# Product 2 of batch 0 moved in front of the rows of batch 2, in the hand-written order of an attention and expert kernel

## The chip, the cores and the metric

The kernel runs on one core of a Trainium2 chip. A core has five engines that run side by side, each through a queue of its own and in order: TensorE (PE, matrix products and transposes), VectorE (DVE), ScalarE (ACT), GpSimd (POOL) and SyncE (SP, which only issues transfers here). They meet through semaphores. The metric is the device time of one execution in microseconds; lower is better.

## The reference, cut to what matters

Four batches of 512 tokens with 512 features go through a normalisation, an int8-quantised two-layer block with weights of the batch's own, a residual, a second normalisation, and a mixture of 8 experts of which each token uses 2, with another residual.

```python
def _smooth_quant_linear(x, w):
    s = sqrt(max(amax_x, EPS) / max(amax_w, EPS))          # per column, over the rows
    xs, ws = x / s, w * s
    x_scale = max(max(abs(xs), axis=-1), EPS) / 127.0      # per row
    w_scale = max(max(abs(ws), axis=-1), EPS) / 127.0
    return round(xs / x_scale) @ round(ws / w_scale).T * x_scale * w_scale.T

def _expert_forward(xe, guw, dw):                          # batch b: guw 512x512, dw 512x256
    gate, up = split(_smooth_quant_linear(xe, guw), 2)     # product 1
    return _smooth_quant_linear(silu(gate) * up, dw)       # product 2

x = x + vmap(_expert_forward)(layernorm(x), w1, w2)
# then x + FFN(layernorm(x)): top 2 of 8 experts by router scores, f32, 512 -> 256 -> 512
```

## The kernel before

**Two parts on one time axis.** The first part quantises and multiplies each of the four batches. The second sorts the tokens by expert into 39 tiles of 128 rows, gathers each tile's rows, multiplies them by its expert's weights and adds the result to the output by an indirect transfer. The expert weights (8 experts, 3 matrices each, so 24 pieces numbered 0 to 23) come in while the first part runs. Each is loaded into one of three staging buffers ("load expert k" on SyncE), its high half is written as f16 by ScalarE ("high k", line 1047), and the rest as bf16 by GpSimd ("low k", line 580), which waits for that high half. "Load expert k" waits until "low k-3" has freed the buffer.

**Steps of a batch b, first linear layer.** "normalise 1 b" (ScalarE, line 1002); "w1 columns b" and "x columns b": TensorE transposes (lines 1166, 1177) and VectorE takes the maxima of the columns (line 722); "root 1 b": GpSimd makes the smoothing factors from them (lines 604 to 608); "rows 1 b": TensorE spreads them and their inverse over the partitions (line 1186), and ScalarE copies one of the two rows ("row_s", line 1015); "smooth w1 b" (GpSimd, line 615) and "smooth x b" (VectorE, line 764) multiply; "w1 scales b" and "x scales b" (VectorE, lines 752 to 756) are the row maxima; "w1 up b" and "x up b" (ScalarE, line 1032) scale and round; "w1 transposed b" and "x transposed b" (TensorE line 1177, then ScalarE line 1041) turn the operands; "w1 scale row b" (TensorE line 1186, ScalarE line 1015); "product 1 b" (TensorE line 1205, VectorE line 781).

**Second linear layer.** "silu b" and "gate times up b" (ScalarE line 1053, GpSimd line 627) make its input; then the same steps with names in 2, w2 and a, and "product 2 b" (TensorE line 1205, VectorE line 790). GpSimd adds it to the input ("residual b", line 644). From there come "moments 2", "normalise 2", the transposed tokens (line 1217) and the router's scores (line 1228).

**What sets the order.** Each engine has a table of step names with a batch or tile number (SP_ORDER, POOL_ORDER, DVE_ORDER, ACT_ORDER, PE_ORDER), and the steps are issued exactly in that order. Each step starts with its own semaphore waits, so a step that waits holds up all behind it on its engine. In POOL_ORDER, "low 9" to "low 12" stand between "deviation 1 2" and "root 1 2"; that table isn't touched. PSUM banks are used in rings of one or two, in the order in which TensorE's table fills them.

**Fillers.** FILLERS gives a number of matmuls with a result that nobody reads, issued at the start of a step, after it has its bank and before it waits for its input (`keep_busy`, line 1154).

The names that the tables and the change use are defined in the functions at lines 1166 to 1205 (TensorE), 1002 to 1062 (ScalarE), 722 to 790 (VectorE) and 580 to 644 (GpSimd). The lines that put the fillers ahead of the wait, and a low behind its high, are:

```python
                for c in range(n):
                    bank = ring.fill(pe, stage, c, b)
                    if c == 0:
                        keep_busy(bank, stage, b)
                        pe.wait_ge(ready, count * (b + 1))
...
            def low(k):
                hi, lo = parts(k)
                pool.wait_ge(sem("hi_done"), k + 1)
                pool.tensor_tensor(lo, staged(k), hi, ALU.subtract).then_inc(sem("lo_done"), 1)
```

Of the kernel before, what the change touches and what calls it, by code (L numbers as in the profile page):

```python
# [32 lines left out]
def in_order(text):  # L33


    return [(entry.rsplit(" ", 1)[0], int(entry.rsplit(" ", 1)[1])) for entry in text.split(", ")]
# [22 lines left out]
DVE_ORDER = in_order(  # L59
# [12 lines left out]
ACT_ORDER = in_order(  # L72
# [15 lines left out]
PE_ORDER = in_order(  # L88
# [16 lines left out]


FILLERS = {
    ("w1 columns", 0): 9, ("x columns", 0): 4, ("rows 1", 0): 2, ("w1 scale row", 0): 30, ("rows 1", 1): 3,
    ("rows 2 inverse", 0): 18, ("w1 transposed", 1): 6, ("rows 1", 2): 6, ("product 2", 0): 8, ("sort step", 0): 5,
    ("sort step", 1): 3, ("sort step", 2): 3, ("sort step", 3): 3,  # L110
}

# [1266 lines left out]
```

## Time and profile before

| | us |
|---|---|
| median of 3 runs | 383.69 (383.41 to 383.95) |
| the profiled execution, whole | 383.51 |
| its span in the profile | 381.8 |
| TensorE busy | 324.1 (85%) |
| GpSimd busy | 244.6 (64%) |
| VectorE busy | 222.9 (58%) |
| ScalarE busy | 205.4 (54%) |
| mean granted clock of TensorE | 0.978 of full |

The profile is of one execution. "Busy" is the time in which an engine works on an instruction, without its waits. A timeline row gives start, duration, engine, source line and operation, written tile and read tiles, and in brackets how long the engine stood idle before it and which instruction ended that. In these names w_in is the tile of w1 or of w2 (512 or 256 columns tell which), row_w and row_s are rows spread over the partitions, bank_t, bank_r, bank_q and bank_h are PSUM. The granted clock is 1.00 at 2.4 GHz and 0.50 at 1.2 GHz.

### The profile page before, as it was taken

To read this page: it belongs to the slowest core of one execution; us is meant where nothing else is said; L and a number is where in the kernel's file an instruction comes from. 1 tells how busy PE (TensorE), PEld (TensorE's weight loads), DVE (VectorE), ACT (ScalarE), POOL (GpSimd) and SP (SyncE) were. 2 spreads that over 40 slices of the span, in tenths; PEclk is the share of its full clock that TensorE was granted. 3 is DMA by queue.
4 is the path that set the end of the run, shared out by engine and by line. 5 is a ranking of instruction groups with operands and counts; after the bars stand their busy time and mean duration, and the time that the engine had idled before them with its cause. 6 is when DMAs were issued, how large, how long until landed. Compare 5 with 4: busy or idle time off the path is not lost.

```text
span 381.8 us, 6238 instructions
## 1 busy us (share of the span) xinstructions
PE 324.1 (85%) x1837; PEld 192.2 (50%) x1863; DVE 222.9 (58%) x511; ACT 205.4 (54%) x386; POOL 244.6 (64%) x271
## 2 busy tenths in 40 slices
PE   5796868877897885679998899999999999999980
PEld 2454525545665752365574354555555555555540
DVE  3685887778889989887678733333333333333320
ACT  1559568878899597138636234444444444444430
POOL 6485697879899972486371462546667756675441
PEclk9999969998999999999999999999999999999996
DMA  7764545743766417255318545456777657786543
GB/s 248 250 251 150 178 165 169 267 173 118 286 230 248 167 55 192 89 176 188 127 12 293 83 140 85 86 108 99 150 129 114 122 104 120 135 130 105 98 55 58
DMA packets 27552, 56.80 MB, mean 149 GB/s; under 512 B 2624, under 2 KB 13888, under 8 KB 25600
## 3 DMA queue, kind: packets, MB, share of 16 engines
q0 software_dynamic: 8736, 20.45, 29.4%
q1 hardware_dynamic: 17968, 35.39, 26.9%
q10 hardware_dynamic: 816, 0.54, 0.4%
q8 instruction: 18, 0.29, 0.3%
q14 instruction: 14, 0.11, 0.1%
HBM read 37.50 MB, written 18.87 MB: 148 GB/s over the span
## 4 chain that ended last, share of the span: by engine, by line
PE 46%; DVE 15%; POOL 15%; issue 12%; ACT 6%; DMA 3%; POOLq 1%; SPq 0%; DVEq 0%; ACTq 0%
PE bank_h L1311 19%; PE bank_q L1332 9%; PE bank_t L1296 4%; DVE amax L722 4%; PE bank_q L1177 3%; POOL x L644 3%; POOL w_in L662 2%; DVE xn L764 2%; DVE rmax L752 2%; POOL out L683 2%; PE bank_r L1154 2%; PE bank_h L1205 2%; PE bank_r L1322 2%; DMA stage<-tokens,gather_at 2%; ACT xn L1002 2%
## 5 line engine op out<-in xcount | busy, mean ns | idle before, releaser
L1311 PE MATMUL bank_h<-gu_hi,xT 128*128 x312 | 103.9, 379 | 0.7
L958 DVE SCALAR_TENSOR_TENSOR xT<-bank_t,xT 128x512 f16<-128x512 f32 x39 | 26.8, 690 | 54.2 <-ACT xT L1090 54.2
L1332 PE MATMUL bank_q<-dn_hi,aT 128*128 x156 | 52.6, 379 | 1.9 <-DVE aT L976 1.4
L1311 PE MATMUL bank_h<-gu_lo,xT 128*128 x142 | 53.8, 379 | 0.0
L1311 PEld LDWEIGHTS bank_h<-gu_hi,xT 128*128 128x128 f16 x312 | 30.5, 98 | 29.3 <-issue 0.2
L580 POOL TENSOR_TENSOR gu_lo<-stage,gu_hi 128x1024 bf16<-128x1024 f32 x16 | 34.0, 2136 | 12.2 <-ACT gu_hi L1047 12.0
L662 POOL DMA_INDIRECT w_in<-tokens,gather_at x30 | 29.8, 993 | 17.8 <-issue 7.6
L1097 ACT ACTIVATE gated<-bank_h 128x256 f32<-128x256 f32 x39 | 15.0, 385 | 37.9 <-PE bank_h L1311 37.9
L966 DVE SCALAR_TENSOR_TENSOR gated<-bank_h,gated 128x256 f32<-128x256 f32 x39 | 16.5, 423 | 32.1 <-ACT gated L1097 32.1
L722 DVE TENSOR_REDUCE amax<-bank_t 128x1 f32<-128x512 f32 x48 | 30.9, 685 | 6.6 <-PE bank_t L1177 4.4
L683 POOL DMA_INDIRECT out<-h,scatter_at x17 | 26.9, 1580 | 12.1 <-DMA out<-h,scatter_at 4.7
L683 POOL DMA_INDIRECT out<-xn,scatter_at x16 | 25.2, 1575 | 11.6 <-ACT xn L1119 10.1
L1104 ACT ACTIVATE aT<-bank_r 128x256 f16<-128x256 f32 x39 | 14.8, 383 | 27.0 <-PE bank_r L1322 25.8
L976 DVE TENSOR_TENSOR aT<-bank_r,aT 128x256 f16<-128x256 f32 x39 | 16.3, 423 | 20.4 <-ACT aT L1104 20.4
L1090 ACT ACTIVATE xT<-bank_t 128x512 f16<-128x512 f32 x39 | 23.1, 592 | 9.4 <-PE bank_t L1296 9.1
L1332 PE MATMUL bank_q<-dn_lo,aT 128*128 x73 | 27.7, 379 | 0.0
L1332 PEld LDWEIGHTS bank_q<-dn_hi,aT 128*128 128x128 f16 x156 | 15.2, 97 | 22.3 <-issue 8.1
L284 POOL TENSOR_TENSOR hold_p<-identf 128x1 f32<-128x1 f32 x30 | 11.1, 371 | 20.6 <-SPq L517 18.3
L644 POOL TENSOR_TENSOR x<-x,xn 128x512 f32<-128x512 f32 x16 | 19.8, 1275 | 4.2 <-DVE xn L790 4.1
L1311 PEld LDWEIGHTS bank_h<-gu_lo,xT 128*128 128x128 f16 x156 | 15.2, 98 | 11.3
L1119 ACT ACTIVATE h<-bank_q,slot_weight 128x512 f32<-128x512 f32 x17 | 11.7, 687 | 15.1 <-PE bank_q L1332 15.1
L1119 ACT ACTIVATE xn<-bank_q,slot_weight 128x512 f32<-128x512 f32 x16 | 11.0, 688 | 15.3 <-PE bank_q L1332 15.3
(196 smaller groups left out, 716.9 us busy)
## 6 DMA issues: line engine op xcount, KB each, us to landing
stage<-in_L_ffn_gate_proj SPq DMA_DIRECT2D x8, 512.0 KB, 4.3
stage<-in_L_ffn_up_proj SPq DMA_DIRECT2D x8, 512.0 KB, 4.3
stage<-in_L_ffn_down_proj SPq DMA_DIRECT2D x8, 512.0 KB, 4.8
x<-in_x SPq DMA_DIRECT2D x4, 1024.0 KB, 6.3
out<-x SPq DMA_DIRECT2D x4, 1024.0 KB, 4.6
tokens<-xn SPq DMA_DIRECT2D x4, 1024.0 KB, 5.3
x_in<-in_x SPq DMA_DIRECT2D x3, 1024.0 KB, 5.9
w_in<-in_fside_BxS2xS SPq DMA_DIRECT2D x3, 1024.0 KB, 5.4
```

What stands on the lines that cost most here:

```text
L580: pool.tensor_tensor(lo, staged(k), hi, ALU.subtract).then_inc(sem("lo_done"), 1)
L644: pool.tensor_tensor(x1[:, j], x1[:, j], xn2[:, j], ALU.add).then_inc(sem("x1_ready"), 1)
L662: pool.indirect_dma_start(out=xg(i), out_offset=None, in_=rows, in_offset=bass.IndirectOffsetOnAxis(ap=gather_at[:, i:i + 1], axis=0)).the ...
L683: pool.indirect_dma_start(out=out, out_offset=bass.IndirectOffsetOnAxis(ap=scatter_at[:, i:i + 1], axis=0), in_=y(i), in_offset=None, comp ...
L722: dve.tensor_reduce(amax[which][:, b % 2, side, c, 0:1], bank, AX.X, ALU.max, apply_absolute_value=True).then_inc(ring_t.taken, 1)
L958: dve.scalar_tensor_tensor(out=xT[i % 2][:, 1].rearrange("p c t -> p (c t)"), in0=bank, scalar=X_SCALE, in1=xT[i % 2][:, 0].rearrange("p c ...
L966: dve.scalar_tensor_tensor(out=gated[i % 2][:], in0=bank[:, F:2 * F], scalar=A_SCALE / X_SCALE, in1=gated[i % 2][:], op0=ALU.mult, op1=ALU ...
L976: dve.tensor_tensor(aT[i % 2][:, 1].rearrange("p c t -> p (c t)"), bank[:, 0:F], aT[i % 2][:, 0].rearrange("p c t -> p (c t)"), ALU.subtra ...
L1090: act.activation(xT[i % 2][:, 0].rearrange("p c t -> p (c t)"), bank, ACT.Copy, scale=X_SCALE).then_inc(sem("x_high"), 1)
L1119: act.activation(y(i), bank, ACT.Identity, scale=slot_weight[:, i:i + 1]).then_inc(ring_q.taken, 1)
L1311: ins = pe.matmul(bank, xT[i % 2][:, part, c], rhs[:, cols], start=(c == 0 and m == 0), stop=(c == C - 1 and m == 2))
L1332: ins = pe.matmul(bank, aT[i % 2][:, part, c], rhs[:, cols], start=(c == 0 and n == 0), stop=(c == FC - 1 and n == 2))
```

## The change

Only tables of the order and the constants of the fillers change. Product 2 of batch 0, with the transposes and evacuations that feed it, moves in front of "rows 1 2" on TensorE and ScalarE and in front of "smoothing 1 2" on VectorE. On ScalarE "high 9" to "high 12" go behind it. GpSimd's and SyncE's tables stay. One line of the VectorE table, and the constants:

```diff
-    "x columns 2, smoothing 1 2, moments 1 3, smooth x 2, w1 scales 2, product 2 0, x scales 2, a columns 1, "
+    "w1 columns 2, x columns 2, product 2 0, smoothing 1 2, moments 1 3, smooth x 2, w1 scales 2, x scales 2, "
...
 FILLERS = {
     ("w1 columns", 0): 9, ("x columns", 0): 4, ("rows 1", 0): 2, ("w1 scale row", 0): 30, ("rows 1", 1): 3,
-    ("rows 2 inverse", 0): 18, ("w1 transposed", 1): 6, ("rows 1", 2): 6, ("product 2", 0): 8, ("sort step", 0): 5,
+    ("rows 2 inverse", 0): 18, ("w1 transposed", 1): 6, ("rows 1", 2): 2, ("product 2", 0): 3, ("w1 transposed", 2): 22, ("sort step", 0): 5,
     ("sort step", 1): 3, ("sort step", 2): 3, ("sort step", 3): 3,
 }
```

ScalarE, from the evacuation of "x transposed 1" on, before:

```order
L1041 ACTIVATE xqT<-bank_q 128x512 x4
L1047 ACTIVATE gu_hi<-stage 128x4x256 x2
L1002 ACTIVATE xn<-x_in,shift,rstd 128x512 x4
L1047 ACTIVATE dn_hi<-stage 128x1024
L1047 ACTIVATE gu_hi<-stage 128x4x256
L1032 ACTIVATE w_in<-w_in,inv 128x256 x4
L1041 ACTIVATE dqT<-bank_q 128x512 x2
L1015 ACTIVATE row_w<-bank_r 128x512
L1015 ACTIVATE row_s<-bank_r 128x512
L1032 ACTIVATE av<-av,inv 128x256 x4
L1047 ACTIVATE gu_hi<-stage 128x4x256
L1041 ACTIVATE aqT<-bank_q 128x512 x2
```

The same place with the change:

```order
L1041 ACTIVATE xqT<-bank_q 128x512 x4
L1002 ACTIVATE xn<-x_in,shift,rstd 128x512 x4
L1032 ACTIVATE w_in<-w_in,inv 128x256 x4
L1032 ACTIVATE av<-av,inv 128x256 x4
L1041 ACTIVATE dqT<-bank_q 128x512 x2
L1041 ACTIVATE aqT<-bank_q 128x512 x2
L1015 ACTIVATE row_w<-bank_r 128x512
L1047 ACTIVATE gu_hi<-stage 128x4x256 x2
L1047 ACTIVATE dn_hi<-stage 128x1024
L1047 ACTIVATE gu_hi<-stage 128x4x256
L1015 ACTIVATE row_s<-bank_r 128x512
L1047 ACTIVATE gu_hi<-stage 128x4x256
```

The four highs, 9 to 12 (gu_hi twice, dn_hi, gu_hi), stood around "normalise 1 2", and now stand behind the evacuations of batch 0 (dqT, aqT, row_w) and in front of row_s, which is "rows 1 2".

TensorE, from "w1 columns 2" on, before:

```order
L1166 MATMUL bank_t<-identf,w_in 128x128 x16
L1177 MATMUL bank_t<-identf,xn 128x128 x16
L1177 MATMUL bank_q<-identf,w_in 128x128 x8
L1186 MATMUL bank_r<-identf,scale 128x128 x4
L1154 MATMUL bank_r<-number,below 128x512 x6
L1186 MATMUL bank_r<-identf,smooth 128x128 x8
L1177 MATMUL bank_q<-identf,av 128x128 x8
L1154 MATMUL bank_h<-number,below 128x512 x8
L1205 MATMUL bank_h<-dqT,aqT 128x512 x8
L1186 MATMUL bank_r<-identf,scale 128x128 x4
L1177 MATMUL bank_q<-identf,w_in 128x128 x16
L1177 MATMUL bank_t<-identf,av 128x128 x8
```

With the change:

```order
L1166 MATMUL bank_t<-identf,w_in 128x128 x16
L1177 MATMUL bank_q<-identf,w_in 128x128 x8
L1177 MATMUL bank_q<-identf,av 128x128 x8
L1177 MATMUL bank_t<-identf,xn 128x128 x16
L1186 MATMUL bank_r<-identf,scale 128x128 x4
L1154 MATMUL bank_h<-number,below 128x512 x3
L1205 MATMUL bank_h<-dqT,aqT 128x512 x8
L1154 MATMUL bank_r<-number,below 128x512 x2
L1186 MATMUL bank_r<-identf,smooth 128x128 x8
L1186 MATMUL bank_r<-identf,scale 128x128 x4
L1154 MATMUL bank_q<-number,below 128x512 x22
L1177 MATMUL bank_q<-identf,w_in 128x128 x16
```

The transposes of w2 and av now stand in front of "x columns 2" (xn into bank_t), the product (bank_h) in front of "rows 1 2" (smooth), and 22 fillers on bank_q stand between "w1 scale row 2" (scale) and "w1 transposed 2".

## Rows read from the trace of the kernel before

**Rows 1.** The chain that ended last, shares of the span by engine.
```profile
PE 46%; DVE 15%; POOL 15%; issue 12%; ACT 6%; DMA 3%; POOLq 1%; SPq 0%; DVEq 0%; ACTq 0%
```

**Rows 2.** Windows view: busy us of each engine, granted clock, DMA share, GB/s.
```profile
98.70:136.60 37.90, 31.82 (x230) 24.55 (x232) 34.80 (x76) 31.46 (x58) 36.65 (x31) 1.00 0.60 215
```

**Rows 3.** Timeline of ScalarE: start us, us, engine, line, operation, count, [idle before].
```profile
66.75 1.99 ACT L1047 ACTIVATE gu_hi<-stage 128x1024 f16<-128x1024 f32 x2
68.64 2.92 ACT L1002 ACTIVATE xn<-x_in,shift,rstd 128x512 f32<-128x512 f32 x4
...
73.50 1.06 ACT L1047 ACTIVATE gu_hi<-stage 128x1024 f16<-128x1024 f32 x1 [1.00 <-DMA stage<-in_L_ffn_gate_proj]
74.47 1.69 ACT L1032 ACTIVATE w_in<-w_in,inv 128x256 f32<-128x256 f32 x4
...
77.99 0.60 ACT L1015 ACTIVATE row_w<-bank_r 128x512 f32<-128x512 f32 x1
```

**Rows 4.** Timeline of GpSimd, 60 to 160 us.
```profile
67.87 4.24 POOL L580 TENSOR_TENSOR gu_lo<-stage,gu_hi 128x1024 bf16<-128x1024 f32 x2 [3.02 <-ACT gu_hi L1047]
...
77.62 0.20 POOL L604 TENSOR_TENSOR ratio<-ratio,clamped 128x4 f32<-128x4 f32 x1 [0.81 <-DVE clamped L725]
...
97.39 0.20 POOL L604 TENSOR_TENSOR ratio<-ratio,clamped 128x2 f32<-128x2 f32 x1 [0.87 <-DVE ratio L733]
...
156.12 2.49 POOL L627 TENSOR_TENSOR av<-h 128x512 f32<-128x512 f32 x2 [10.50 <-PE bank_q L1177]
```

**Rows 5.** Timeline of TensorE, 73 to 78 us.
```profile
73.71 1.26 PE L1177 MATMUL bank_t<-identf,xn 128*128 128x128 f32 x8 [0.19 <-DVE amax L722]
...
76.38 1.04 PE L1177 MATMUL bank_q<-identf,w_in 128*128 128x128 f32 x8
77.26 0.60 PE L1186 MATMUL bank_r<-identf,scale 128*128 128x128 f32 x4
```

**Rows 6.** Timeline of TensorE, 59 to 64 us.
```profile
59.68 1.46 PE L1154 MATMUL bank_q<-number,below 128*128 128x512 f16 x6
60.98 1.04 PE L1177 MATMUL bank_q<-identf,w_in 128*128 128x128 f32 x8
...
63.67 1.15 PE L1177 MATMUL bank_q<-identf,xn 128*128 128x128 f32 x8 [0.20 <-ACT wqT L1041]
```

**Rows 7.** Timeline of SyncE's queue; from the page, DMA issues with us to landing.
```profile
70.04 0.37 SPq L490 DMA_DIRECT2D stage<-in_L_ffn_gate_proj  x1
...
stage<-in_L_ffn_gate_proj SPq DMA_DIRECT2D x8, 512.0 KB, 4.3
...
x_in<-in_x SPq DMA_DIRECT2D x3, 1024.0 KB, 5.9
```

**Rows 8.** Timeline of ScalarE, 87 us.
```profile
87.45 2.56 ACT L1032 ACTIVATE w_in<-w_in,inv 128x512 f32<-128x512 f32 x4 [0.39 <-DVE inv L756]
```

**Rows 9.** Timeline of VectorE, 87 us.
```profile
87.33 2.19 DVE L790 SCALAR_TENSOR_TENSOR xn<-bank_h,scale,row_w 128x512 f32<-128x512 f32 x3
```

**Rows 10.** Timeline of TensorE, 88 to 94 us.
```profile
88.13 1.69 PE L1205 MATMUL bank_h<-dqT,aqT 128*128 128x512 bf16 x4 [2.12 <-DVE xn L790]
89.61 1.06 PE L1186 MATMUL bank_r<-identf,scale 128*128 128x128 f32 x4
90.47 3.25 PE L1177 MATMUL bank_q<-identf,w_in 128*128 128x128 f32 x16
93.55 1.04 PE L1177 MATMUL bank_t<-identf,av 128*128 128x128 f32 x8
```

**Rows 11.** Windows view at the edges of the half-clock stretches.
```profile
51.00:51.50 0.50, 0.00 (x0) 0.00 (x0) 0.50 (x2) 0.50 (x1) 0.50 (x1) 0.77 0.99 410
58.00:58.50 0.50, 0.50 (x4) 0.20 (x2) 0.50 (x2) 0.50 (x2) 0.50 (x1) 0.90 0.91 244
88.50:89.00 0.50, 0.45 (x3) 0.13 (x2) 0.46 (x2) 0.50 (x2) 0.42 (x2) 0.82 0.62 117
92.00:92.50 0.50, 0.50 (x4) 0.23 (x3) 0.50 (x1) 0.31 (x2) 0.50 (x1) 0.77 0.00 0
```

54 rows, old and new, of tables (ACT_ORDER, DVE_ORDER, PE_ORDER) are left out of this document.

## The prediction

> **What bounds the kernel now.** I read the chain that ended last first [rows 1]: TensorE has 46% of it, VectorE and GpSimd 15% each. No engine holds it throughout, so what counts is who is full in the stretch behind the change. The windows view tells: from 98.7 to 136.6 us GpSimd is busy for 36.65 of 37.90 us, VectorE for 34.80, TensorE for 31.82 [rows 2]. So GpSimd has almost no slack there, and whatever makes it late at 98.7 makes everything late by that much. The change sits just ahead of that stretch, so I then read the four engines' timelines from 60 to 100 us, then the clock.
>
> **What moves.** On GpSimd nothing: its order and SyncE's are unchanged. On ScalarE "high 9" to "high 12" (two of them at 66.75 us, the last at 73.50 us) go behind "w2 scale row 0" [rows 3]. On TensorE the transposes of product 2 of batch 0 go between "w1 columns 2" and "x columns 2", the product in front of "rows 1 2". On VectorE "product 2 0" goes in front of "smoothing 1 2".
>
> **Step 1: GpSimd's stall.** GpSimd runs "low 9" to "low 12" before "root 1 2", and each low waits for its high. Before, "low 9" starts at 67.87 us, 1.12 us behind the high at 66.75 [rows 3, 4], and "root 1 2" follows at 77.62 us, having waited 0.81 us for VectorE [rows 4]. After, ScalarE first does "normalise 1 2" (2.92 us, from 66.75 instead of 68.64) and the two scale-ups (1.69 us a piece) [rows 3], ready by about 73 us, when TensorE ends "w1 columns 2" and would have begun "x columns 2" (73.71 us, after 0.19 us of waiting, so free at some 73.4) [rows 5]. Its four new transpose groups take some 2.5 us: the four groups of the row at 60.98 us need 2.69 us to the next stage's start, 0.20 of it a wait that "x columns 2", in other banks, doesn't have [rows 6]. So "x columns 2" starts at 75.9 us. It holds TensorE 2.67 us (73.71 to 76.38), the scale row is evacuated 0.73 us after its start (77.26 to 77.99) [rows 3, 5], and the next ScalarE instruction follows 0.5 us on (0.60 us, less the 0.1 us by which neighbours on ScalarE overlap: 66.75 + 1.99 against 68.64): "high 9" at 79.8 us, "low 9" at 80.9 us. That is 13.0 us later than before.
>
> Two lows take 4.24 us [rows 4], so 9, 10 and 11 end at 87.3 us. "high 12" needs its load, which SyncE issues when "low 9" has freed the buffer: 70.04 us before, 3.46 us ahead of "high 12" [rows 3, 7]; now 83.05 us, so "high 12" at 86.5, "low 12" at 87.6 and "root 1 2" at 89.85 us. **Delay 12.2 us.** With a load of 4.3 us, the median that the page gives for such loads, it would be 13.0. "Load x 3" stands behind that load in SyncE's queue and now goes out at 83.4 us; with 5.9 us to landing [rows 7] it is there at 89.3, just before "moments 1 3" (now some 91.6 us), so it costs nothing; it has 2 us of cover. VectorE's "x columns 2", 1.7 to 2.2 us late, and "product 2 0" behind it (done by about 83 us) hide in the same stall.
>
> **Step 2: down to the scales.** Queued behind "root 1 2" are "smooth w1 2" on GpSimd, "smooth x 2" and "w1 scales 2" on VectorE, and "w1 up 2" on ScalarE, which waits for the scales to the end (87.45 us, 0.39 us idle) [rows 8]. "Low 13", "gate times up 1" and "residual 0" follow on GpSimd and are late by the same. None is shortened by the change, so they start 12.2 us late: the scales are there at 99.6 us.
>
> **Step 3: what the move gives back.** "Product 2 0" held VectorE from 87.33 us, three instructions in 2.19 us and a fourth of 0.73, ahead of "x scales 2" [rows 9]; TensorE waited 2.12 us for it and only then did "w1 scale row 2" at 89.61 us [rows 10]. Both go. On its own that is worth at most the 2.2 us from 87.4 to 89.6 us on TensorE; step 4 takes it.
>
> **Step 4: the 22 fillers.** They run between "w1 scale row 2" and "w1 transposed 2", before its wait. "w1 up 2" would be ready at about 102.2 us. At full clock a filler takes 0.217 us (six between 59.68 and 60.98 us) [rows 6]: 99.6 + 0.43 + 22 x 0.217 = 104.8 us. TensorE stands idle from about 82 to 91 us, and but for 1 us again until 99.6. In the trace far shorter gaps go with the half clock: the granted clock falls to 0.50 at about 51.2 us, while TensorE is idle, and is back at 58.05, some 6.8 us; it falls again at 88.8, behind the 2.12 us gap, and is back at 92.2 us, 3.4 us [rows 10, 11]. These are the levels 2.4 and 1.2 GHz. At half clock four scale transposes take 0.86 us instead of 0.43 [rows 5, 10], so a filler takes twice 0.217, 0.43 us. With 3.4 us of half clock from 99.6: scale row to 100.5, six fillers to 103.0, sixteen more to 106.5 us. With 6.8 us: 108.2 us. Against 90.47 us before [rows 10] that is +16.0 or +17.7; at full clock throughout +14.3. "w1 transposed 2" itself ran mostly at half clock, 3.08 us to the next stage (90.47 to 93.55) [rows 10], and four groups at full clock take 2.69 [rows 6]: 0.4 back.
>
> The Trainium skill ("TensorE: Matmul & The Clock Gate", What's actually happening) says that the lower clock is the default and activity releases it; by that rule fillers after so long a gap begin at the lower level, which speaks against the +14.3 case and against fillers as a cure that costs nothing. The trace agrees in kind, since one half-clock stretch begins in a gap, the other behind one, and both end while TensorE is busy; that the clock has fallen by 99.6 us no row can show.
>
> So "a columns 1" starts 15.6 to 17.3 us late (13.9 at full clock). I take 16.2, nearer the shorter stretch because TensorE is busy without a break there, as in the second one. "Root 2 1" on GpSimd, which before waited 0.87 us for VectorE's column maxima [rows 4], waits for them longer: its own queue would be there at +12.2 - 0.87 = +11.3 us. From there GpSimd is full [rows 2] and hands the delay on.
>
> **The other edits.** Fillers of "rows 1 2" from 6 to 2 and of "product 2 0" from 8 to 3 fall in the gap of step 1: nothing. Highs 13 to 15 and their loads lie in the wait for the scales (about 92 to 99 us): nothing; should that cover fail, ScalarE would be late by a high, about 1 us.
>
> **Sum.** +12.2 (stall) + 4.0 (fillers beyond the wait, less what steps 3 and 4 give back) = +16.2 us. The profiled execution took 383.5 us (its span 381.8), the median of the runs is 383.7, so 0.2 us apart: 399.7 us.
>
> **Rivals.** (a) Stalled, but the fillers cost little: TensorE keeps its clock or the maxima are not what "root 2 1" waits for. Then GpSimd's queue decides, +11.3 us, 394.8 us, up to 397.4 with 22 fillers at full clock. For it: behind the 2.12 us gap the clock still stood at 1.00 for 0.7 us; against it: the gap is now about four times as long. (b) Not slower, by absorption behind: GpSimd has 10.50 us of idle time before 156.12 us [rows 4], waiting for TensorE. If that stretch, which orders batches 0 and 1, did not depend on batch 2's chain, the delay would be eaten there, and the clock and the gap of step 3 would be a gain: 383.5 - 2.2 - 1.7 (half of the 3.4 us at half clock) = 379.6 us. It decides only when all of 16 us is absorbed. Against it: the ranking needs the scores of batch 1, these its residual, and that stands behind "root 2 1" in GpSimd's full queue. (c) A longer chain: slow load (0.8) and the 6.8 us of half clock (1.1) together give +18.1, 401.6 us. (d) "Low 9" is not the gate, because something else of the order frees GpSimd: then the scales are late only by TensorE's 2.2 us of new transposes, 89.6 us, the fillers end at 94.8 instead of 90.47, and +4.3 - 0.4 = +3.9 us stays, 387.4 us. The queues are in order, so I give it little.
>
> **How the numbers follow.** The forecast (within 397.4 to 401) 0.62; (a) 0.17; (c) 0.10; (b) 0.06; (d) 0.05. The range 394.0 to 402.5 takes in the forecast, (a) and (c), 0.89 of the chance, of which some 0.05 may lie beyond its ends. About 0.2% is what a measurement of this kernel can tell from no change. Faster comes from (b), 0.04; the same from a partial (b), 0.02; slower 0.94.
>
> **What would show it.** GpSimd idle for some 15 us up to about 80.9 us, released by ScalarE's "gu_hi"; "root" for batch 2 about 12 us late; 22 fillers on bank_q partly at half clock; a second GpSimd idle of 4 to 6 us before "root 2 1"; then all stages shifted by one constant to the end. Wrong would be: the first low before 78 us, a shift that shrinks behind 140 us, or fillers hidden under "w1 up 2".

## The result and the profile after

The changed kernel takes 399.14 us (median; 398.73 to 399.50), beside 383.82 us (383.41 to 384.34) of the kernel before in the same comparison: the ratio is 1.040 [1.0367, 1.0427], 15.3 us slower. The forecast was 399.7 us. The profiled execution took 398.73 us, its span is 396.9, and the mean granted clock fell from 0.978 to 0.959.

All times below are the trace's own. Before the first moved instruction this execution is 0.42 us ahead of the one of before (normalise 1 2 would start at 66.75 us, the time of the high that it displaces [rows 3], and starts at 66.33). Up to there the two kernels issue the same instructions; but TensorE of before worked at half clock from 51.3 to 58.1 us, and in this execution the clock stayed at 1.00 there. Here are the same 18 fillers of TensorE near 52 us, of before and then of after:

```profile
52.27 6.92 PE L1154 MATMUL bank_r<-number,below 128*128 128x512 f16 x18 [1.71 <-DVEq L766]
```

```profile
52.42 4.06 PE L1154 MATMUL bank_r<-number,below 128*128 128x512 f16 x18 [1.71 <-DVEq L766]
```

I say where this head start matters.

GpSimd first (start us, us, engine, line, operation, written and read tiles, count, idle before and what ended it), from the timeline of 60 to 200 us:

```profile
79.94 4.21 POOL L580 TENSOR_TENSOR gu_lo<-stage,gu_hi 128x1024 bf16<-128x1024 f32 x2 [14.94 <-ACT gu_hi L1047]
...
86.55 2.12 POOL L580 TENSOR_TENSOR gu_lo<-stage,gu_hi 128x1024 bf16<-128x1024 f32 x1 [0.31 <-ACT gu_hi L1047]
88.62 0.20 POOL L604 TENSOR_TENSOR ratio<-ratio,clamped 128x4 f32<-128x4 f32 x1
...
111.56 0.20 POOL L604 TENSOR_TENSOR ratio<-ratio,clamped 128x2 f32<-128x2 f32 x1 [3.60 <-DVE ratio L733]
...
171.69 2.49 POOL L627 TENSOR_TENSOR av<-h 128x512 f32<-128x512 f32 x2 [11.90 <-PE bank_q L1177]
```

These answer to [rows 4]. The first row is the stall: GpSimd idles 14.94 us for ScalarE's gu_hi, where it had idled 3.02. "Low 9" is 12.07 us later. "Root 1 2" (third row) is 11.0 us later, "root 2 1" (fourth) 14.17 us, after a second idle of 3.60 us for VectorE. The last row is 15.57 us later: between the fourth and the fifth another 1.4 us were lost, which nothing in the prediction has.

ScalarE, and SyncE's queue below it, show why the low is late (same columns, 60 to 128 us):

```profile
66.33 2.92 ACT L1002 ACTIVATE xn<-x_in,shift,rstd 128x512 f32<-128x512 f32 x4
...
78.32 0.60 ACT L1015 ACTIVATE row_w<-bank_r 128x512 f32<-128x512 f32 x1 [2.31 <-PE bank_r L1186]
78.81 1.99 ACT L1047 ACTIVATE gu_hi<-stage 128x1024 f16<-128x1024 f32 x2
...
85.41 1.06 ACT L1047 ACTIVATE gu_hi<-stage 128x1024 f16<-128x1024 f32 x1 [3.66 <-DMA stage<-in_L_ffn_gate_proj]
```

```profile
82.10 0.37 SPq L490 DMA_DIRECT2D stage<-in_L_ffn_gate_proj  x1
82.51 0.51 SPq L458 DMA_DIRECT2D x_in<-in_x  x1
```

Against [rows 3]: "normalise 1 2" has the highs' place. The scale row's evacuation (78.32) comes 2.31 us after ScalarE was free, waiting for TensorE, and highs 9 and 10 follow it at once. The load for expert 12 goes out at 82.10 us, when the first of the two lows has freed the buffer, and ScalarE waits 3.66 us for it to land before "high 12".

TensorE from 60 to 128 us, which answers to [rows 5] and [rows 10]:

```profile
75.21 1.04 PE L1177 MATMUL bank_t<-identf,xn 128*128 128x128 f32 x8
...
90.29 1.97 PE L1186 MATMUL bank_r<-identf,smooth 128*128 128x128 f32 x8 [8.31 <-POOL smooth L608]
98.56 1.08 PE L1186 MATMUL bank_r<-identf,scale 128*128 128x128 f32 x4 [6.30 <-DVE inv L756]
99.44 6.11 PE L1154 MATMUL bank_q<-number,below 128*128 128x512 f16 x22
105.39 1.04 PE L1177 MATMUL bank_q<-identf,w_in 128*128 128x128 f32 x8
...
107.72 1.04 PE L1177 MATMUL bank_t<-identf,av 128*128 128x128 f32 x8
```

The second row is TensorE waiting 8.31 us for the smoothing of the late root, the third 6.30 us for the scales. The 22 fillers then take 5.95 us until "w1 transposed 2" at 105.39, which was at 90.47 [rows 10]: +14.9 us. At full clock 22 would take 4.8 us (22 x 0.217 [rows 6]). "W1 transposed 2" is over in 2.33 us, and "a columns 1" at 107.72 is 14.17 us late, the same 14.17 that GpSimd's "root 2 1" shows.

VectorE (60 to 128 us), against [rows 9]:

```profile
79.47 2.86 DVE L790 SCALAR_TENSOR_TENSOR xn<-bank_h,scale,row_w 128x512 f32<-128x512 f32 x4 [0.70 <-PE bank_h L1205]
90.27 0.18 DVE L742 RECIPROCAL smooth<-smooth 128x4 f32<-128x4 f32 x1 [7.94 <-POOL smooth L608]
...
108.36 1.29 DVE L722 TENSOR_REDUCE amax<-bank_t 128x1 f32<-128x512 f32 x2 [7.29 <-PE bank_t L1177]
```

Product 2 (four instructions, 2.86 us) is done at 82.3 us, eight before the smoothing at 90.27: it hides in the stall. The last row is the column maxima for which "root 2 1" waits.

The windows view (stretch, length, then busy us of TensorE, weight loads, VectorE, ScalarE, GpSimd, granted clock, DMA share, GB/s) gives the edges of the half clock, as [rows 11] did:

```profile
84.50:85.00 0.50, 0.00 (x0) 0.00 (x0) 0.00 (x0) 0.00 (x0) 0.50 (x1) 0.79 1.29 434
...
101.50:102.00 0.50, 0.50 (x3) 0.21 (x2) 0.00 (x0) 0.00 (x0) 0.50 (x2) 0.64 1.09 383
102.00:102.50 0.50, 0.50 (x4) 0.23 (x3) 0.00 (x0) 0.00 (x0) 0.50 (x1) 1.00 1.09 373
163.00:163.50 0.50, 0.32 (x2) 0.00 (x0) 0.50 (x1) 0.50 (x2) 0.00 (x0) 0.80 0.76 197
170.00:170.50 0.50, 0.50 (x4) 0.34 (x3) 0.38 (x3) 0.00 (x0) 0.00 (x0) 0.87 0.04 16
```

The clock goes from 1.00 to 0.50 (2.4 to 1.2 GHz) near 84.8 us, in TensorE's long idle time, and comes back at 101.86, 3.3 us after TensorE resumed with the scale row at 98.56. It falls again at 163.3 and is back by 170.1. That is the sort of batch 0. Before, its four steps were 2.17 us apart, and now some are 2.78 apart; here are two steps of each kernel (TensorE, 142 to 158 us of before, 158 to 173 us of after):

```profile
147.81 0.85 PE L1267 MATMUL bank_r<-packed,onehot 128*128 128x384 f16 x4 [2.34 <-DVE packed L875]
...
149.98 0.85 PE L1267 MATMUL bank_r<-packed,onehot 128*128 128x384 f16 x4 [0.83 <-DVE packed L875]
```

```profile
161.98 0.85 PE L1267 MATMUL bank_r<-packed,onehot 128*128 128x384 f16 x4 [2.33 <-DVE packed L875]
...
164.15 1.46 PE L1267 MATMUL bank_r<-packed,onehot 128*128 128x384 f16 x4 [0.83 <-DVE packed L875]
```

The same four matmuls take 0.85 us in the first step of both, and in the second 0.85 us before and 1.46 us after. The wait ahead of the first is the same too, 2.34 and 2.33 us. From GpSimd's "gap" at 152.14 us to the last row of the first fence it is 19.55 us; before it was 18.16 (137.96 to 156.12). Here are the missing 1.4 us.

### The profile page after: what moved, and what is told of

The parts are those of the page before. It is cut to its first block, busy times and chain, and to the rows that moved or that the text cites. A ratio compares the mean times of both kernels' runs of the same rounds, so it can differ in the third digit from the quotient of the medians.

```text
span 396.9 us, 6263 instructions
## 1 busy us (share of the span) xinstructions
PE 328.7 (83%) x1850; PEld 194.3 (49%) x1876; DVE 223.4 (56%) x511; ACT 205.2 (52%) x386; POOL 244.8 (62%) x271
## 4 chain that ended last, share of the span: by engine, by line
PE 42%; POOL 18%; DVE 15%; issue 13%; ACT 7%; DMA 3%; POOLq 2%; SPq 0%; DVEq 0%; ACTq 0%
PE bank_h L1311 17%; PE bank_q L1332 8%; PE bank_t L1296 3%; PE bank_q L1177 3%; POOL x L644 3%; POOL gu_lo L580 3%; DVE rmax L752 3%; DVE amax L722 3%; POOL w_in L662 2%; POOL out L683 2%; ACT w_in L1032 2%; DVE xn L764 2%; POOL dn_lo L580 2%; PE bank_r L1267 2%; DMA stage<-tokens,gather_at 2%
## 5 line engine op out<-in xcount | busy, mean ns | idle before, releaser
L722 DVE TENSOR_REDUCE amax<-bank_t 128x1 f32<-128x512 f32 x48 | 30.9, 685 | 14.7 <-PE bank_t L1177 12.2
L1311 PEld LDWEIGHTS bank_h<-gu_lo,xT 128*128 128x128 f16 x156 | 15.3, 98 | 11.3
L1119 ACT ACTIVATE h<-bank_q,slot_weight 128x512 f32<-128x512 f32 x17 | 11.7, 687 | 15.1 <-PE bank_q L1332 13.2
L615 POOL TENSOR_TENSOR w_in<-w_in,row_s 128x1024 f32<-128x1024 f32 x8 | 17.3, 2182 | 3.5 <-ACT row_s L1015 3.4
```

Of the source, the lines that this page charges most:

```text
L615: pool.tensor_tensor(rows, rows, spread(row_s1[:], [P, J // 2, D], 1), ALU.mult).then_inc(sem("ws_ready"), 1)
L722: dve.tensor_reduce(amax[which][:, b % 2, side, c, 0:1], bank, AX.X, ALU.max, apply_absolute_value=True).then_inc(ring_t.taken, 1)
L1311: ins = pe.matmul(bank, xT[i % 2][:, part, c], rhs[:, cols], start=(c == 0 and m == 0), stop=(c == C - 1 and m == 2))
```

## The experiments

Each is told with its edit, against the kernel that it starts from ("after" or "before"), what was expected of it, and what came. Ratios are to the kernel before, run beside it, whose medians were 383.5 to 384.0 us.

**The stall alone, and the fillers alone.** Both start from before.

```diff
 ACT_ORDER (before)
-high 9, high 10, normalise 1 2, high 11, high 12, w2 up 0, w2 transposed 0, w2 scale row 0
+normalise 1 2, w2 up 0, w2 transposed 0, w2 scale row 0, high 9, high 10, high 11, high 12
```

> The kernel before with one edit: high 9 to high 12 behind w2 scale row 0 on ScalarE. Product 2 of batch 0 and the constants stay as before. Theory (the stall of GpSimd alone costs what it cost in the changed kernel): low 9 near 79.6 us, root 1 2 near 88.6 us, 11 us late, and all behind it by the same: 394 to 396 us. Rival (the stall is hidden if TensorE and VectorE keep their old order, and the loss comes from product 2 standing in front of the rows): under 386 us.

Measured: 395.76 us (394.42 to 396.07), ratio 1.030 [1.0255, 1.0349], +12.2 us. GpSimd of this kernel, 60 to 200 us:

```profile
79.28 4.20 POOL L580 TENSOR_TENSOR gu_lo<-stage,gu_hi 128x1024 bf16<-128x1024 f32 x2 [14.19 <-ACT gu_hi L1047]
...
107.58 0.19 POOL L604 TENSOR_TENSOR ratio<-ratio,clamped 128x2 f32<-128x2 f32 x1 [0.15 <-DVE ratio L733]
...
167.87 2.48 POOL L627 TENSOR_TENSOR av<-h 128x512 f32<-128x512 f32 x2 [11.95 <-PE bank_q L1177]
```

With nothing else of the change, "low 9" waits 14.19 us and "root 2 1" comes 10.2 us late almost without waiting (0.15 us). The last row is 11.75 us late, since here too the sort falls to half clock: from "gap" (148.25) to it there are 19.62 us instead of 18.16, 1.5 us more. The stall is most of the loss.

```diff
 FILLERS (before)
-("rows 1", 2): 6,
+("rows 1", 2): 6, ("w1 transposed", 2): 22,
```

> The kernel before with one edit: 22 fillers in front of w1 transposed 2. Theory (they are exposed wherever w1 up 2 is ready before they end): they start at 90.5 us, four of them at half clock, the rest at 0.217 us, and w1 transposed 2 starts at 96.1 instead of 90.5 us, less 0.4 us from the full clock: 388 to 389.5 us. Rival (they run in a wait and keep the clock up, which pays for them): 382.5 to 384.5 us.

Measured: 386.95 us (386.04 to 388.25), ratio 1.009 [1.0064, 1.0122], +3.4 us. TensorE, 60 to 128 us:

```profile
82.62 3.24 PE L1154 MATMUL bank_h<-number,below 128*128 128x512 f16 x8
...
89.09 4.91 PE L1154 MATMUL bank_q<-number,below 128*128 128x512 f16 x22
93.84 1.04 PE L1177 MATMUL bank_q<-identf,w_in 128*128 128x128 f32 x8
```

The 22 fillers put "w1 transposed 2" at 93.84 instead of 90.47 [rows 10]. They ran at full clock, since the half clock in this execution stood at 83 to 86.4 us, over the fillers of "product 2 0" (82.62: eight in 3.24 us). The time lies 1 us below the expected range, in part for this reason. The two medians' losses, 12.2 and 3.4, add up to 15.6 us, and the whole change costs 15.3. The interval of each leaves 1 to 2 us of play. Some of the agreement is chance too: all three traces have a fall of the clock in the sort (1.5 us with the highs alone, 0.6 with the fillers alone, 1.4 in the change), which the sum counts twice.

**The fillers within the change.** None, and six, where the change has 22.

```diff
 FILLERS (after)
-("w1 transposed", 2): 22,
```

> The changed kernel without the 22 fillers in front of w1 transposed 2. Theory (they last 5.9 us where the wait they stand in is 2.4 us): w1 transposed 2 starts at about 101.1 us, when w1 up 2 is done, at half clock; its four groups need 3.2 instead of 2.3 us, and root 2 1 comes at 108 to 109 us instead of 111.6, as GpSimd's own queue is free at 108. Time 395.6 to 396.5 us. Rival (the fillers pay for themselves, since without them the half clock goes on through the stages behind): 398 to 401 us.

Measured: 397.26 us (396.89 to 397.43), ratio 1.035 [1.0308, 1.0394]: 1.9 us less than with 22, and 0.8 us above the expected range. TensorE (60 to 128 us), one row of the windows view, and GpSimd:

```profile
101.29 3.80 PE L1177 MATMUL bank_q<-identf,w_in 128*128 128x128 f32 x16 [1.50 <-ACT w_in L1032]
```

```profile
106.00:107.00 1.00, 1.00 (x6) 0.67 (x4) 0.84 (x2) 1.00 (x3) 1.00 (x2) 0.50 0.73 82
```

```profile
109.44 0.19 POOL L604 TENSOR_TENSOR ratio<-ratio,clamped 128x2 f32<-128x2 f32 x1 [1.35 <-DVE ratio L733]
```

Without them "w1 transposed 2" starts at 101.29 us, 4.1 us earlier, but all sixteen matmuls run at half clock (3.80 us), which lasts to 107 us instead of 101.86. "Root 2 1" is only 2.1 us earlier. So in these two executions the fillers shorten the half clock, and cost twice what they return. The sort falls to half clock here too (19.77 us from "gap" to "gate times up 3"), for which the expectation had no term.

```diff
 FILLERS (after)
-("w1 transposed", 2): 22,
+("w1 transposed", 2): 6,
```

> The changed kernel with 6 instead of 22 fillers in front of w1 transposed 2. Theory (a few fillers fill the wait for w1 up 2 and start the return of the clock, the other 16 only cost): fillers until about 102 us at half clock, w1 transposed 2 at 102.0, clock back by about 103, a columns 1 at 105 us, root 2 1 at 108.5 to 109.2 us: 395.8 to 396.8 us. Rival (only the whole of 22 brings the clock back, six leave the half clock until 107 us as with none): 397.3 to 398.2 us.

Measured: 396.81 us (395.39 to 397.74), ratio 1.032 [1.0261, 1.0372]. TensorE, 60 to 128 us:

```profile
99.30 2.77 PE L1154 MATMUL bank_q<-number,below 128*128 128x512 f16 x6
101.86 1.64 PE L1177 MATMUL bank_q<-identf,w_in 128*128 128x128 f32 x8
```

Six take 2.56 us to the next stage's start, at half clock, and "w1 transposed 2" begins 0.6 us later than without fillers; "root 2 1" comes at 108.52 us. By the ranges of their times six and none can't be told apart, and both are better than 22.

**Highs back in front.** Does the stall go when ScalarE's highs go back, with the rest of the change in place?

```diff
 ACT_ORDER (after)
-normalise 1 2, w2 up 0, a up 0, w2 transposed 0, a transposed 0, w2 scale row 0, high 9, high 10, high 11, high 12
+high 9, high 10, normalise 1 2, high 11, high 12, w2 up 0, a up 0, w2 transposed 0, a transposed 0, w2 scale row 0
```

> The changed kernel with high 9 to high 12 put back on ScalarE where they stood before (9 and 10 ahead of normalise 1 2, 11 and 12 behind it); everything else of the change stays, the 22 fillers too. Theory (GpSimd waits for the highs, and that stall is 11 of the 15 us): low 9 starts near 67.5 us again and root 1 2 no longer waits for lows. It now waits for the column maxima, since the two scale-ups come behind four highs and TensorE holds x columns 2 back behind the transposes that need them: root 1 2 near 82 us, product 2 0 on VectorE until 85, scales of w1 near 93 us instead of 98.4, then 22 fillers mostly at full clock. Time 390 to 393 us. Rival (what counts is TensorE's new order and the fillers, the highs are hidden): 398 to 400 us, as the changed kernel.

Measured: 397.87 us (397.26 to 398.31), ratio 1.037 [1.0325, 1.0415]: a miss by 5 us, nearly as slow as the change. "Low 9" was in time (68.10 us). TensorE, the windows view and GpSimd:

```profile
76.52 1.38 PE L1177 MATMUL bank_q<-identf,w_in 128*128 128x128 f32 x8 [2.77 <-ACT w_in L1032]
...
80.27 3.81 PE L1177 MATMUL bank_t<-identf,xn 128*128 128x128 f32 x16
```

```profile
78.00:84.00 6.00, 5.49 (x25) 5.02 (x26) 2.07 (x3) 2.13 (x4) 0.00 (x0) 0.50 0.48 172
```

```profile
85.15 0.20 POOL L604 TENSOR_TENSOR ratio<-ratio,clamped 128x4 f32<-128x4 f32 x1 [8.13 <-DVE clamped L725]
```

TensorE's queue has the transposes of product 2 ahead of "x columns 2". With the highs first, the scale-ups are late, TensorE waits for them (2.77 us in the first row), its clock falls, and the stage behind "x columns 2" starts at 83.88 us, where it had started at 76.38 [rows 5]; "root 1 2" waits 8.13 us for VectorE instead of for a low. My expectation had put back one side of a crossing of two queues and left the other. The clock is the second part of the miss: I had expected the 22 fillers mostly at full clock, and in this execution it was at 0.50 from 94.2 to 101.0 us, so that they took 6.42 us.

**Both constraints at once, in two ways.** First the highs where each has slack, then TensorE's columns in front of the transposes. Both without the 22 fillers.

```diff
 ACT_ORDER (after, and no fillers at "w1 transposed" 2)
-normalise 1 2, w2 up 0, a up 0, w2 transposed 0, a transposed 0, w2 scale row 0, high 9, high 10, high 11, high 12
+high 9, high 10, normalise 1 2, high 11, w2 up 0, a up 0, w2 transposed 0, a transposed 0, high 12, w2 scale row 0
```

> The changed kernel without the 22 fillers, and with the highs spread over ScalarE so that neither GpSimd nor TensorE waits long: high 9 and 10 ahead of normalise 1 2, high 11 behind it, high 12 between a transposed 0 and w2 scale row 0. Product 2 of batch 0 stays in front of the rows of batch 2 on all engines. Theory (what is left is the price of the early product itself: x columns 2 about 2.6 us late on TensorE, and 2.9 us of product 2 on VectorE in front of smoothing 1 2): root 1 2 at 80.5 us, scales of w1 at 92.2, a columns 1 at 98 us, 387 to 389.5 us. Rival (the early product pays once the stall is gone): 380.5 to 383.5 us.

Measured: 391.82 us (390.87 to 392.53), ratio 1.020 [1.0148, 1.0256]: 2.3 us above the range.

```diff
 PE_ORDER (after, no fillers at "w1 transposed" 2)
-w2 transposed 0, a transposed 0, x columns 2, w2 scale row 0
+x columns 2, w2 transposed 0, a transposed 0, w2 scale row 0
 ACT_ORDER (after): the highs as in "Highs back in front"
```

> The changed kernel without the 22 fillers, high 9 to 12 as in the kernel before, and x columns 2 in front of the transposes of product 2 on TensorE; product 2 still stands in front of the rows of batch 2 on TensorE and in front of smoothing 1 2 on VectorE. Theory (VectorE decides: product 2 can't be ready before the scale-ups behind the four highs, and smoothing 1 2 waits behind it): root 1 2 on time near 77.6 us, product 2 on VectorE from 81 to 84 us, smoothing 1 2 at 84 instead of 79.3, scales of w1 at 92 us: 389.5 to 392 us, as the run with the highs spread out. Rival (x columns being late on TensorE was the cost): under 387 us.

Measured: 389.97 us (389.21 to 392.52), ratio 1.015 [1.0118, 1.018], in the range. VectorE of the first and of the second kernel, 60 to 128 us (the line numbers of the second are one lower):

```profile
81.31 2.86 DVE L790 SCALAR_TENSOR_TENSOR xn<-bank_h,scale,row_w 128x512 f32<-128x512 f32 x4 [0.70 <-PE bank_h L1205]
84.09 0.17 DVE L742 RECIPROCAL smooth<-smooth 128x4 f32<-128x4 f32 x1
```

```profile
81.28 2.86 DVE L789 SCALAR_TENSOR_TENSOR xn<-bank_h,scale,row_w 128x512 f32<-128x512 f32 x4 [3.57 <-PE bank_h L1204]
84.06 0.17 DVE L741 RECIPROCAL smooth<-smooth 128x4 f32<-128x4 f32 x1
```

"Root 1 2" starts at 80.95 us in the first and at 77.86, as before, in the second, yet the smoothing (second row of each) starts at 84.1 in both, without idle time. It is the product that it stands behind. Before, smoothing came at 79.3 us and the scales at 87.4; now the scales are there at 92.2. So with "root 1 2" on time the kernel still loses 6.0 us by the median. Of these 4.8 are there at the scales, because the early product puts 2.9 us of VectorE's work, and the wait for TensorE ahead of it, on the path to them. The rest comes later: "root 2 1" is 5.7 us late (103.09), behind a half clock from 87.2 to 100.8 us, and the sort of this execution lost 0.8 us more. It was also the slowest of the four (392.52 us, the others 389.21 to 390.43). Behind the scales, where it stood, it kept TensorE waiting 2.12 us [rows 10].

**The second half clock, in the sort.** Nine more of the fillers that stand behind "w2 transposed 2", ahead of the wait for the first sort step.

```diff
 FILLERS (after)
-("sort step", 0): 5,
+("sort step", 0): 14,
```

> The changed kernel with 14 instead of 5 fillers in front of the first step of the sort of batches 0 and 1, where TensorE waits 2.33 us for VectorE and where the changed kernel's clock falls behind the wait (163.2 to 169.9 us at half clock; the kernel before has full clock there). Theory (that half-clock stretch is what turned a delay of 14.2 us at GpSimd's root 2 1 into 15.6 us at gate times up 3, since each of three sort steps took 2.78 instead of 2.17 us): nine more fillers, 1.95 us, end just ahead of the wait's end, the clock stays up, 397.4 to 398.0 us. Rival (the 1.4 us come from elsewhere, or the clock falls at that time whatever TensorE does): 398.8 to 399.5 us.

Measured: 397.91 us (397.55 to 398.72), ratio 1.036 [1.0307, 1.0415], 1.2 us less than the change. TensorE, 158 to 173 us:

```profile
159.02 3.19 PE L1261 MATMUL bank_r<-number,below 128*128 128x512 f16 x14
162.60 0.85 PE L1267 MATMUL bank_r<-packed,onehot 128*128 128x384 f16 x4 [0.39 <-DVE packed L875]
...
164.76 0.85 PE L1267 MATMUL bank_r<-packed,onehot 128*128 128x384 f16 x4 [0.83 <-DVE packed L875]
```

The wait shrinks from 2.33 to 0.39 us (second row), the second step takes 0.85 us again, and from "gap" to "gate times up 3" it is 18.17 us, as before. The 1.4 us are the half clock's. In this execution "root 2 1" came at 112.18 us, 0.6 us later than in the change, although the two kernels are the same up to the sort: the clock rose at 103.1 us instead of 101.9, and the 22 fillers, shown here, took 0.6 us longer to the next stage.

```profile
99.46 6.72 PE L1154 MATMUL bank_q<-number,below 128*128 128x512 f16 x22
```

**Fillers without the move.** Can the half clock behind TensorE's 2.12 us gap [rows 10, 11] be had more cheaply?

```diff
 FILLERS (before)
-("product 2", 0): 8,
+("product 2", 0): 16,
```

> The kernel before with 16 instead of 8 fillers in front of product 2 of batch 0, so that TensorE's wait of 2.12 us there shrinks to under 0.5 us. Theory (what the change could give back at this place is the half clock from 88.8 to 92.2 us and little else): no half clock from 88 to 92 us, root 2 1 up to 0.9 us earlier, where GpSimd's own queue bounds it; 382.7 to 383.3 us, against 383.6 to 383.8. Rival (nothing to be had: the clock falls anyway, or something else is late next): 383.5 to 384.0 us.

Measured: 384.10 us (382.29 to 387.17), ratio 1.000 [0.9969, 1.0032]. The windows view:

```profile
88.00:92.00 4.00, 2.94 (x18) 1.80 (x19) 3.96 (x6) 3.73 (x7) 3.87 (x5) 1.00 0.83 262
...
148.00:152.00 4.00, 2.81 (x11) 0.90 (x9) 3.06 (x7) 1.50 (x3) 0.00 (x0) 0.61 0.90 258
```

The eight extra fillers fill the gap; the clock stays at 1.00 there, and from "root 1 2" to "root 2 1" it is 18.86 us (77.87 to 96.73) instead of 19.77 [rows 4], 0.91 less. But 60 us later the sort, which had the full clock in before, now falls to 0.61 and 0.53, and gives it back: from "gap" to "gate times up 3" it is 19.81 us instead of 18.16. The medians can't confirm either half of this, since the interval of the ratio takes in both a gain of 0.9 us and none. The expected 382.7 to 383.3 us was missed by 0.8.

So both together:

```diff
 FILLERS (before)
-("product 2", 0): 8, ("sort step", 0): 5,
+("product 2", 0): 16, ("sort step", 0): 14,
```

> The kernel before with two filler constants: 16 instead of 8 in front of product 2 of batch 0 (as in the run with that edit alone) and 14 instead of 5 in front of the first sort step. Theory (the 0.9 us won at root 2 1 were lost again to a half clock in the sort; with that held off they stay): full clock from 60 to 220 us, 382.5 to 383.1 us, ratio 0.997 to 0.9985 to the kernel before. Rival (the gain is taken by something later, a gather or the last tiles): no difference, 383.4 to 384.0 us.

Measured: 381.92 us (381.37 to 383.96), beside 383.95: ratio 0.996 [0.9932, 0.998], 0.6 us below the expected range. It beats both kernels, though by little. GpSimd, 60 to 200 us:

```profile
95.73 0.22 POOL L604 TENSOR_TENSOR ratio<-ratio,clamped 128x2 f32<-128x2 f32 x1
...
154.40 2.49 POOL L627 TENSOR_TENSOR av<-h 128x512 f32<-128x512 f32 x2 [10.50 <-PE bank_q L1177]
```

"Root 2 1" is again 18.86 us behind "root 1 2" (76.87), and from "gap" (136.21) to the last row it is 18.19 us, the full-clock length. That shows 0.9 us. The median says 2.0; 0.75 us of the profiled execution lie before 77 us, where nothing was changed and executions differ. Other executions of before may lose time in the sort, as its profiled one did not. How much of the rest is the fillers' stays open.

The last one joins the two for the changed kernel:

```diff
 FILLERS (after)
-("w1 transposed", 2): 22, ("sort step", 0): 5,
+("w1 transposed", 2): 6, ("sort step", 0): 14,
```

> The changed kernel with 6 instead of 22 fillers in front of w1 transposed 2 and 14 instead of 5 in front of the first sort step. Theory (both filler losses are apart from each other and from the stall): root 2 1 at about 108.5 us instead of 111.6, and no half clock in the sort, 18.2 instead of 19.6 us from the gap of group 0 to gate times up 3: 394.5 to 395.5 us, the 11 us of the stall remain. Rival (the losses overlap, one of the two repairs gives nothing beside the other): 396.3 to 397.5 us.

Measured: 394.18 us (393.64 to 395.44), ratio 1.027 [1.024, 1.0306]. "Root 2 1" is at 108.46 us, 0.70 us of idle before it; from "gap" to "gate times up 3" it is 18.15 us, and the time is 0.3 us below the expected range. That is 5.0 us better than the change, and still 10 us slower than before: what is left is the stall, 10.8 us at "root 1 2".

## Why the prediction was right

The time and the mechanism were right: a late high, a stalled GpSimd, a full stretch behind it that hands the delay on. Its terms were each some way off, in both directions.

**Step 1, the stall: right, 1.2 us too large.** "Low 9" was put at 80.9 us and came at 79.94 (of the 0.96, 0.42 is the earlier start of this execution). "X columns 2" was put at 75.9 and came at 75.21. "High 12" and its load: forecast 86.5, came 85.41, 3.31 us after the issue instead of 3.46. "Root 1 2": 89.85 against 88.62, a delay of 11.0 instead of 12.2. GpSimd idled only 0.31 us for that high, and "load x 3" behind it cost nothing: "moments 1 3" starts at 90.37 us on VectorE, right behind the smoothing. That low 9 is the gate (rival d is out) is shown by the kernel with the highs alone: +12.2 us by the median, of which its trace gives 10.2 to the stall and 1.5 to the sort's clock.

**Step 2: right.** Everything queued behind "root 1 2" moved with it: "w1 up 2" at 98.45 us, 11.0 late.

**Step 3: right in place, wrong in what it means.** The product's instructions left the path from the scales to TensorE. The prediction said that VectorE hides them in the stall, and they did. It did not say that they stand ahead of the smoothing, so that without most of the stall the kernel with the early product is slower too, by 6.0 and 8.3 us in the two kernels that try it (4.8 us of it at the scales).

**Step 4: right in mechanism, the size nearly so.** From the scale row to "w1 transposed 2" I had 6.9 us (99.6 to 106.5) and it took 6.83; I had 3.4 us of half clock and it was 3.3. "W1 transposed 2" itself gave back 0.75 us against the 0.4 of the sum (2.33 us to the next stage, before 3.08). "A columns 1" so came 14.17 us late against 15.6 by the shorter stretch; and of 15.6 to 17.3 I had taken 16.2, which was wrong by 0.6. Rival (a) is out: the clock did not hold, "root 2 1" waited 3.60 us for the maxima (the forecast had 4 to 6), and without the fillers the change is 1.9 us faster. Rival (c) is out: the load was quick and the half clock short.

**Nothing is absorbed: right, but the shift was not constant.** Rival (b) is out: from 111.56 us to 153 us each stage of GpSimd is 14.2 us late, "gap" among them. Then the prediction's last sign failed: it expected one constant to the end, and the sort added 1.4 us by a half clock that it had no term for. By the times of GpSimd's indirect transfers 0.5 us of that was given back behind 193 us, and the span is 15.1 us longer.

So the sum came out by errors that cancel, which is luck: the stall 1.0 us too large at the scale row (99.6 against 98.56), "w1 transposed 2" 0.35, the choice in the range 0.6, together 2.0 us too much (16.2 against 14.17 at "root 2 1"); the sort's clock 1.4 less 0.5, 0.9 us too little. That leaves 16.2 - 2.0 + 0.9 = 15.1 us, the difference of the spans. Whether a fall in the sort belongs to this change or to the single execution the runs don't settle (last section). The sum also mixed its bases: 399.7 is 16.2 on the profiled execution (383.5); on the median of the runs (383.7) it is 399.9.

**Two of my expectations failed by more than 2 us.** That the highs, put back, would give 390 to 393 us: they didn't, because TensorE's new order waits for scale-ups that then come late. That the placed highs would give 387 to 389.5: no. The scales were there at 92.2 us as expected, but "root 2 1" came at 102.25, and "gap" 1.0 us later still, with a half clock from 122.1 to 125.6 us. Five more medians lay outside their ranges, by 0.3 to 1.1 us: no fillers and sixteen fillers above, the fillers alone and the last two kernels below.

## What to carry to other kernels

When a step is moved forward on one engine, list for every engine what it now stands in front of, and follow each of those to the engine that waits for it: here four instructions of about 1 us on ScalarE cost 11 us, because the low halves of GpSimd, which stand in the same queue ahead of "root 1 2", waited for them. A small wait that the move removes (2.12 us) can be less than what the moved work costs where it lands (2.9 us and a wait on VectorE). Put in fillers by the gap that they close and look at the clock of the whole run, not only at the place, and try a quarter of the number: with six instead of 22 the kernel was 2.3 us faster.

## What the runs showed of the clock that I had not expected

The same instructions with the same wait keep the full clock in one execution and lose it in another. In the sort stage the wait ahead of the first step is 2.33 or 2.34 us in ten kernels. In two of them, before and the one with the placed highs, the granted clock stayed at 1.00 (steps 2.17 us apart). In the other eight (the change, highs alone, fillers alone, highs back, no fillers, six fillers, columns first, and before with sixteen fillers at 83 us) the second step took 1.46 us. In all three kernels with fourteen sort fillers, which leave a wait of 0.39 or 0.40 us, the clock stayed.

That before with sixteen fillers lost the clock there, and before did not, doesn't show that the eight extra fillers at 83 us caused it. Each kernel has one profiled execution, and executions differ with nothing changed. Up to 66 us all thirteen kernels issue the same instructions; yet near 52 us, behind the same wait of 1.7 us, the clock is at 0.50 for 6.8 us in before, for 3.4 us in nine kernels, and not at all in three (the change, highs alone, placed highs). The mean granted clock of the executions of before runs from 0.970 to 0.983, that of the kernel with sixteen fillers from 0.970 to 0.982. What decides it in the sort the runs don't tell.

How long the half clock goes on after TensorE resumes with the scale row differs in the same way. With 22 fillers in one piece behind it, it was 3.3 us in the change (98.56 to 101.86), 4.3 with the highs back, and 4.5 in the kernel that differs from the change only in the sort; with six 4.6 and 4.7; without fillers, with 1.50 us of idle time in it, 5.9 (placed highs), 8.3 and 8.5 us. So the fillers do shorten it, but by how much can't be read from two executions.
